# Four graph layers on one core: the first transposition of each group by VectorE 32x32 blocks and a DMA round trip

## The reference

```python
h = relu(layernorm(x))
# phase 0, two layers: u = (h @ (W_left h)^T above and on the diagonal, h @ (W_right h)^T below) / sqrt(384)
#   h = relu(LN(normalised(exp(u) * adj) @ (h W_lin^T + b)))
# phases 1 and 2, attention, 12 heads of 32:
#   out = softmax(q k^T / sqrt(384) + bias(adj)) v Wo^T + bo
# phase 3, two layers: a = softmax(h h^T / sqrt(384)) * adj, normalised
#   ctx = upper(a) (h Wl^T) + diag(a) (h Ws^T) + lower(a) (h Wr^T);  h = relu(LN(ctx))
x = x + result
```

## Time and profile before

| what | value |
|---|---|
| median of 3 runs | 2790.49 us (2787.36 to 2801.08) |
| span of the profiled execution | 2789.9 us; the page gives no time around it |
| VectorE, ScalarE, GpSimd busy | 2039.2, 1286.7, 1455.7 us (73%, 46%, 52%) |
| DMA queue q1 | 157.88 MB, 17.3% of 16 engines' span, mean 57 GB/s |
| ScalarE's copy of a transposed group (L684, L1558) | 813 and 810 ns |
| GpSimd L1084 (`out`) and L1067 (`xb`), four per group | 865 and 609 ns each |

### The profile page before, as it was taken

One profiled execution on the slowest core, in us unless ns is written; L12 is line 12 of the kernel. 1 busy time (PEld: TensorE's weight loads), 2 busy tenths in 40 slices (PEclk: granted clock), 3 DMA queues, 4 the chain that ended last, 5 costly groups with the idle time before them and its releaser, 6 DMA issues.

```text
span 2789.9 us, 85742 instructions
## 1 busy us (share of the span) xinstructions
PE 2736.0 (98%) x34344; PEld 2535.4 (91%) x34344; DVE 2039.2 (73%) x4000; ACT 1286.7 (46%) x2069; POOL 1455.7 (52%) x2499
## 2 busy tenths in 40 slices
PE   9999999999999999999989999998999999999998
PEld 8999999999988999999889999998888888888887
DVE  5666666666687777777777777778667777777776
ACT  4343343433444444445444444444545545445453
POOL 2212221122225555555554555555677877778777
PEclk9999999999999999999999999999999999999999
DMA  3221111212112111111131111111112112111121
GB/s 122 77 83 41 63 61 41 83 41 67 58 55 85 49 49 49 52 52 49 39 107 46 52 49 49 49 49 64 39 39 75 38 41 72 38 62 51 38 75 35
DMA packets 116556, 159.19 MB, mean 57 GB/s; under 512 B 8048, under 2 KB 112368, under 8 KB 116464
## 3 DMA queue, kind: packets, MB, share of 16 engines
q1 hardware_dynamic: 116464, 157.88, 17.3%
HBM read 107.52 MB, written 50.33 MB: 57 GB/s over the span
## 4 chain that ended last, share of the span: by engine, by line
PE 90%; DVE 4%; POOL 2%; issue 2%; ACT 1%; DMA 1%; SPq 0%; POOLq 0%; DVEq 0%; ACTq 0%
PE ps L337 68%; PE ps L1863 3%; PE ps L1337 3%; PE ps L1319 3%; PE ps L935 3%; PE ps L1352 3%; PE ps L958 2%; PE ps L1841 2%; PE ps L871 2%; PE ps L1247 1%; PE ps L1780 1%; POOL wide L1511 1%; PE ps L1849 0%; DVE w_lo L409 0%; DVE wide L1198 0%
## 5 line engine op out<-in xcount | busy, mean ns | idle before, releaser
L337 PE MATMUL ps<-w_hi,split 128*128 128x384 f32 x4608 | 1267.1, 344 | 9.8 <-ACT wide L1113 5.3
L337 PEld LDWEIGHTS ps<-w_hi,split 128*128 128x128 f32 x4608 | 841.0, 189 | 28.7 <-ACT wide L1113 5.7
L337 PE MATMUL ps<-split,w_hi 128*128 128x256 f32 x4608 | 858.6, 282 | 0.6 <-ACT wide L682 0.6
L337 PE MATMUL ps<-w_lo,split 128*128 128x384 f32 x2304 | 780.2, 339 | 0.0
L337 PEld LDWEIGHTS ps<-split,w_hi 128*128 128x128 f32 x4608 | 719.7, 188 | 20.4 <-issue 19.6
L337 PE MATMUL ps<-split,w_lo 128*128 128x256 f32 x2304 | 583.2, 282 | 0.0
L337 PEld LDWEIGHTS ps<-w_lo,split 128*128 128x128 f32 x2304 | 434.9, 189 | 2.5 <-issue 2.1
L337 PEld LDWEIGHTS ps<-split,w_lo 128*128 128x128 f32 x2304 | 433.6, 188 | 1.3 <-issue 1.2
L1084 POOL TENSOR_TENSOR wide<-wide 128x192 f32<-128x192 f32 x256 | 214.0, 865 | 372.1 <-ACT wide L1147 372.1
L1511 POOL TENSOR_TENSOR wide<-wide,row 128x192 f32<-128x192 f32 x512 | 328.9, 676 | 22.2 <-ACT wide L1594 21.6
L651 POOL TENSOR_TENSOR rstd<-mv,pos_half 128x2 f32<-128x2 f32 x64 | 45.9, 725 | 439.4 <-DVE mv L835 439.4
(11 more groups left out here) (141 smaller groups left out, 4534.8 us busy)
## 6 DMA issues: line engine op xcount, KB each, us to landing
x_after<-wide SPq DMA_DIRECT2D x96, 384.0 KB, 2.5
xin<-x_after SPq DMA_DIRECT2D x96, 384.0 KB, 3.4
xin<-in_x SPq DMA_DIRECT2D x32, 384.0 KB, 4.1
wide<-in_x SPq DMA_DIRECT2D x32, 384.0 KB, 3.6
wide<-x_after SPq DMA_DIRECT2D x32, 384.0 KB, 4.1
out<-wide SPq DMA_DIRECT2D x32, 384.0 KB, 2.8
adjin<-in_adj SPq DMA_DIRECT2D x32, 256.0 KB, 3.7
w_raw<-in_w SPq DMA_DIRECT2D x3, 2304.0 KB, 11.4
```

The lines of the kernel that those rows point to most:

```text
L337: mm = nc.tensor.matmul(out, t if tokens_stay else w, w if tokens_stay else t, start=(k == 0), stop=(k == len(pairs) - 1))
```

## The change

Only the very first group of all is still transposed by PE (stage `first`). For every other group:

1. x is loaded in two DMAs (one per tile) in another order of rows: partition = graph and token within 32, so that tile t holds tokens 32 t to 32 t + 31 of each half; the mean and variance do not care. For attention x is loaded a second time for `xb`, in the old order.
2. `norm` writes h in chunks of 32 features into the place `m.normal()`.
3. VectorE's new stage `turn` transposes all 32x32 blocks of the 128x768 tile in one instruction, back into `xin`.
4. SP stores that tile to HBM (`bounce`), waits for it, and loads it back in four DMAs of 96 KB, one per quarter of the partitions, with the quarters in swapped places (rows of 768 bytes). That gives features on partitions: `hT0`.
5. `split_0` (and `hT` in attention) wait for that DMA and read `hT0` from SBUF. The PE stages `hT_0` and `hT`, and the ScalarE copies behind `hT_0`, are gone. `u_0` reads `hT0`.

```diff
+        def turn(s, i):
+            b = bufs[s]
+            dve.wait_ge(act_done[s], AC[s]("h", i))
+            nc.vector.transpose(b.turned, b.h_all).then_inc(dve_done[s], 1)
...
+    def swap_quarters(s, i):
...
+        sp.wait_ge(now.dve_done[s], now.DV[s]("turned", i))
+        sp.dma_start(g.bounce[s], g.turned[s][:]).then_inc(now.sems.bounced[s], 16)
+        sp.wait_ge(now.sems.bounced[s], 16 * (i + 1))
+        for k in range(QUARTERS):
+            rows = slice(k * HD, (k + 1) * HD)
+            sp.dma_start(now.bufs[s].hT0_rows[rows], g.bounce_quarter[s][k]).then_inc(now.sems.hT_in[s], 16)
...
+    def turn(i):
+        for s in range(STREAMS):
+            store_and_reload(s, i - 2)
+            swap_quarters(s, i)
+            tokens(s, i + 1)
+            adjacency(s, i)
...
         def hT(s, i):
             b = bufs[s]
 
-            act.wait_ge(pe_done[s], PE[s].all(i, ("hT", 0), ("q", 1), ("k", 1), ("v", 1)))
...
-            nc.scalar.activation(b.t_hi[:], b.ps_row2, ACT.Copy).then_inc(act_done[s], 1)
+            act.wait_ge(sems.hT_in[s], QUARTERS * 16 * (i + 1))
...
+            nc.scalar.activation(by_graph(b.t_hi), b.hT0, ACT.Copy).then_inc(act_done[s], 1)
...
-            nc.vector.tensor_tensor(b.t_lo[:], b.ps_row2, b.t_hi[:].bitcast(F32), ALU.subtract)\
+            nc.vector.tensor_tensor(by_graph(b.t_lo), b.hT0, by_graph(b.t_hi).bitcast(F32), ALU.subtract)\
...
-        def hT(s, i):
...
-            for c in range(C):
-                for t in range(T):
-                    mm = nc.tensor.transpose(b.ps_row2[:, c, t * P:(t + 1) * P],
-                                             b.h[:, t, c * P:(c + 1) * P], g.ident[:])
```

The loops now mix three iterations (stages with no, one or two primes), run from iteration 4 to 15 (`MIXED` = 4), and load, normalise and turn a group one iteration before its products. `tokens` waits at a boundary for the store of its own group alone. The lists of all loops and boundaries are new. The attention loop on PE and VectorE:

```diff
-    "q0.1' q1.1' q2.1' k0.1' k1.1' v0.1' v1.1' pt0.0' hT.0 pt1.0' k2a.1' pt2.0' k2bc.1' pv.0' "
-    "scores.1' out0.0' out1.0' q0.0 q1.0 q2.0 k0.0 k1.0 v0.0 v1.0 pt0.1' hT.1 pt1.1' k2a.0 pt2.1' "
-    "k2bc.0 pv.1' scores.0 out0.1' out1.1'",
+    "q0.1'' q1.1'' q2.1'' k0.1'' k1.1'' v0.1'' v1a.1'' pt0.0'' v1bc.1'' pt1.0'' pt2.0'' k2.1'' pv.0'' "
+    "scores.1'' out0.0'' out1.0'' q0.0' q1.0' q2.0' k0.0' k1.0' v0.0' v1a.0' pt0.1'' v1bc.0' pt1.1'' pt2.1'' "
+    "k2.0' pv.1'' scores.0' out0.1'' out1.1''",
...
-    "stat.0 abs.0' fac.0' v.1' hT.0 pv.0' s.1' soft.1' stat.1 abs.1' fac.1' v.0 hT.1 pv.1' s.0 "
-    "soft.0",
-    "bias.1' stat.0 bias.0 p.0' xb.1' out.0' stat.1 p.1' xb.0 out.1'",
+    "abs.0'' fac.0'' v.1'' turn.1' stat.0 hT.0' pv.0'' s.1'' soft.1'' abs.1'' fac.1'' turn.0 stat.1 v.0' "
+    "hT.1' pv.1'' s.0' soft.0'",
+    "bias.1'' bias.0' p.0'' stat.0 out.0'' xb.1'' p.1'' stat.1 xb.0' out.1''",
```

The loop of phase 3 on PE and VectorE begins so, and the beginning on VectorE:

```diff
+    "aT_1.1'' agg_1.0'' u_0.0' w20_1.1'' w21ab_1.1'' w00_0.0' w21c_1.1'' w01_0.0' w10_0.0' w11_0.0' u_0.1' "
...
+    "split_1.1'' soft_1.1'' sum_1.0'' diag_1.0'' att_1.1'' w2_1.0'' aT_1.0'' split_0.0' sum_1.1'' turn.1' "
+    "diag_1.1'' soft_0.0' agg_1.0'' aT_1.1'' w2_1.1'' split_0.1' att_0.0' ln_1.0'' soft_0.1' sum_0.0' "
...
-    "stat.0 w0 split_0.0 w1 stat.1 w2 soft_0.0 att_0.0 split_0.1 lin_0.0 sum_0.0 agg_0.0 w3 ln_0.0 "
+    "stat.0 turn.0 stat.1 split_0.0 w0 w1 w2 turn.1 soft_0.0 att_0.0 w3 split_0.1 lin_0.0 sum_0.0 stat.0+ "
```

More of the change, by code:

```diff
@@ L237, in __call__ @@
         turn = i + self.late[name]
-        if isinstance(turn, int) and turn in (0, ITER):
-            here = sum(self.late[n] == (turn > 0) for n in self.place if self.place[n] <= self.place[name])
-            return here + (ITER * len(self.place) - self.missing if turn else 0)
+        if isinstance(turn, int):
+            whole = sum(min(max(turn - late, 0), ITER) for late in self.late.values())
+            return whole + sum(place <= self.place[name] and 0 <= turn - self.late[n] < ITER
+                               for n, place in self.place.items())
         return turn * len(self.place) + (self.place[name] - self.missing)
@@ L452, in load_x, with adjacency @@
-    def load_x(s, i, of=phase):
-        if of > phase:
-            ph.x_free(sp, s, ITER - 1)
-        elif not isinstance(i, int) or i > 0:
-            ph.x_free(sp, s, i - 1)
-        sp.dma_start(g.xin[s][:], g.sources[of][0][i * STREAMS + s]).then_inc(g.x_in[of][s], 16)
-    def load(s, i, of=phase):
-        load_adj(s, i, of)
-        load_x(s, i, of)
+    def adjacency(s, i):
+        now = ph
+        if isinstance(i, int) and i >= ITER:
+            if nxt == len(phases):
+                return
+            now, i = phases[nxt], i - ITER
+            if i == 0:
+                ph.adj_free(sp, s, ITER - 1)
+        if later(i):
+            now.adj_free(sp, s, i - 1)
+        _, adj, kinds, _ = g.sources[now.phase]
+        sp.dma_start(g.adjin[s][:, 0:len(kinds)], adj[i * STREAMS + s][:, kinds[0]:kinds[-1] + 1:kinds.step])\
+            .then_inc(now.sems.adj_in[s], 16)
@@ new lines, in tokens @@
+    def tokens(s, i):
+        now, made = ph, phases[phase - 1] if phase else None
+        if isinstance(i, int) and i >= ITER:
+            if nxt == len(phases):
+                return
+            now, made, i = phases[nxt], ph, i - ITER
+            if i == 0:
+                ph.x_free(sp, s, ITER - 1)
+                sp.wait_ge(sems.bounced[s], 16 * ITER)
+        if later(i):
+            now.x_free(sp, s, i - 1)
+            sp.wait_ge(now.sems.bounced[s], 16 * i)
+        if made is not None:
+            sp.wait_ge(made.sems.stored[s], 16 * (i + 1) + 1)
+        source = g.sources[now.phase][3] if phase or not very_first(s, i) else g.first_source
+        for t in range(T):
+            sp.dma_start(g.xin[s][:, t], source[i * STREAMS + s][t]).then_inc(now.sems.x_in[s], 16)
@@ L479, in move_program @@
         matrix(1)
[L480 removed]
+        tokens(1, 0)
         matrix(2)
[L482 removed]
+        adjacency(0, 0)
         for dst, src in g.const_loads:
@@ L852, in layer, with first @@
                     f"sum_{l}": total, f"agg_{l}": agg, f"ln_{l}": ln}
-        return {"stat": stat, "gain": gain, "beta": beta, "out": out, **layer(0), **layer(1)}
+        return {"stat": stat, "turn": turn, "gain": gain, "beta": beta, "out": out, **layer(0), **layer(1)}
     def tensor_stages(pe):
+        def first(s, i):
+            b = bufs[s]
+            pe.wait_ge(g.first_tile, 1)
+            for t in range(T):
+                if t > 0:
+                    pe.wait_ge(act_done[s], AC[s]("h", i))
+                for c in range(C):
+                    mm = nc.tensor.transpose(b.rows[0][:, c, t * P:(t + 1) * P], b.h_rows[:, t, c * P:(c + 1) * P], g.ident[:])
+            mm.then_inc(g.first_hT, 1)
+            warm_up(g, BRIDGING)
         def layer(l):
@@ L1271, in stage @@
                         o_taken(s, i, 0)
+                        if started(i, before) and before_att is None:
+                            pe.wait_ge(before.act_done[s], before.AC[s]("z_1", ITER - 1))
                         weights_made(pe, g, phase, WQ, i)
@@ L1761, in layer @@
                     f"aT_{l}": aT, f"agg_{l}": agg, f"ln_{l}": ln}
-        return {"stat": stat, "out": out, **layer(0), **layer(1)}
+        return {"stat": stat, "turn": turn, "out": out, **layer(0), **layer(1)}
     def tensor_stages(pe):
```

350 lines of the change are left out of this document (190 added, 160 removed), and 329 rows, old and new, of tables (BEGINNING, BETWEEN, ENDING, GCN0_ORDERS).

## The result

The changed kernel takes 2804.32 us (median of 5; 2801.59 to 2810.98) against 2790.8 for the kernel before on the same chip: ratio 1.0046, interval 1.0027 to 1.0064. It is 0.5% slower; 2716 was forecast. The profiled execution has a span of 2809.2 us against 2789.9, so the traces show +19.3, where the forecast had -75.

The account below looks back on a forecast made before the run. PE, busy for 98% of the 2789.9 us span, was taken as the bound. 2789.9 - 83.8 + 5 + 0 + 3.3 + 0 = 2714.4, or 2715.0 against the runs' median; 2716 was stated, range 2695 to 2765.

Parts of the forecast that it names:

- Part 1: PE, all phases: 127 blocks of six transpositions go, at 0.66 us each, -83.8 us (bounds -72 and -95).
- Part 2: VectorE gains 127 block transpositions at 0.96 us; its attention loop still fits; +5 us for GpSimd's lateness (bounds 0 and +20).
- the clause on the graph stages: Graph stages: a third to a quarter of VectorE's time is empty, so the block transposition costs nothing in a gap.
- Part 3: Store and four reloads on SP take 6.5 us (bounds 5 and 10), fitting by 0.7 in the last stage: 0.
- Part 4: ScalarE loses 63 copies of 0.81 us; VectorE's t_lo with two SBUF sources stays at 0.96: nothing.
- Part 5: Start: first product +3.0 us, as w0 follows the split; second group's trip +0.3; bounds 2 and 9.
- Part 6: Boundaries between phases: new orders for some 400 stages may shrink or grow 32 us of idle time; 0, bounds -15 and +15.
- It doesn't do what it says: Rival, whole kernel: the round trip's small waits cost what PE saved, time within 0.5%; chance 0.05.
- VectorE took next to nothing from attention: Rival judged here: VectorE becomes the bound in attention, 2758 us (range 2736 to 2775); chance 0.14.
- the trip was not late in the last stage: Rival judged here: at 10 us the trip is late in the last stage, +45 us, 2760; chance 0.08.
- the block transposition does not work block by block: Rival judged here: VectorE's transposition works block by block at 3.9 us, making the kernel slower, 2873 us; chance 0.09.
- the marks named ahead: Signs: 762 transpositions fewer, half-round 16.7, turn at most 0.96, trip 6.5, PE 100% in last stage, first product near 15 us.

Follow-up runs that it names:

- c3_turn_twice: c3_final with VectorE's block transposition issued twice for every group, in all four phases: 2791.29 us, ratio 0.9995.
- x3_order0: The changed kernel with two pairs exchanged in phase 0's lists: hT_1.1 ahead of norm.1, split_1.1 ahead of turn.1; 2802.93 us, ratio 1.0033.
- x4_trip_long: x1_adj_first with one more store to another place in DRAM, waited for, ahead of each trip's own store: 2813.92 us, ratio 1.0065.
- x1_adj_first: The changed kernel with the adjacency's load ahead of the store-and-reload trip and the tokens in each turn of the load program: 2774.44 us, ratio 0.9937.
- c4_cast_order: c3_final with both sides of the first cast in phases 0 and 3 walked in another order: 2746.52 us, ratio 0.9832.
- x2_start: The changed kernel with VectorE's list of the beginning altered, w0 ahead of split_0.0 and stat.1: 2806.3 us, ratio 1.0049.
- c3_final: x1_adj_first plus reordered lists, both first groups transposed on PE, trip before store out of phase 0, one token source corrected: 2743.41 us, ratio 0.9825.

## Why the prediction was wrong

**Part 1 (PE's blocks, -83.8): right in size.** PE's starts give 0.60 us for a group's six transpositions in phase 0 (2.52 to 1.32 for two), 0.655 in attention (1.31 to nothing) and 0.68 in phase 3, against 0.66 taken: 31 x 0.60 + 64 x 0.655 + 32 x 0.68 = 82. In attention the median round fell by 1.33 us, against 1.32 from the blocks alone. The counts fell as forecast: 192 transpositions are left in each graph phase where 384 were, and none of the first kind in attention.

**Part 2 (VectorE in attention, +5): right.** `turn` takes 0.97 us where 0.96 was taken, and the half-round is 16.6 (from 1607.54 to 1624.10 below) where 16.68 was forecast; c3_turn_twice shows the spare time: one half-round grew by the whole 1.00 that was added, so it had nothing to spare, where 0.11 was counted, and the other took 1.0 without growing, where 1.7 was counted.

```profile
1607.54 1.75 DVE L1299 TENSOR_TENSOR wide<-ps,bias 128x1536 f32<-128x1536 f32 x1
1624.10 1.75 DVE L1299 TENSOR_TENSOR wide<-ps,bias 128x1536 f32<-128x1536 f32 x1
```

The Trainium skill, Vector Engine (DVE) Microarchitecture Reference, section 3.8, gave one element per cycle per lane for the block transposition; the trace agrees, as it costs what the two-source operation of the same size does. What failed in this part is the clause on the graph stages, "costs nothing there if the order leaves it in a gap". In phase 0 the order did not: `norm.1` and `turn.1` ahead of the second layer's copy and split cost 0.6 us for a round (x3_order0).

**Part 3 (the trip, 0): the step that failed.** The trip itself was no longer than worked out where it was tightest: in the last stage 5.9 us (median) from the store's issue to the last landing, where 6.5 was taken; 6.4 in attention and 8.1 in phase 0, inside the bounds of 5 and 10. PE never waited for it in loop 3, and x4_trip_long, whose trip is 2.3 us longer there, shows at least that much to spare, where the prediction had 0.7. What failed is one sentence: "Behind the swap SP has `tokens` and `adjacency`, which GpSimd needs later than that." It compared the wrong two times. The adjacency was held above all by the trip's first wait, for VectorE's turn (SP stood 9.5 us at L521 in the rows above), and not by the trip alone, and GpSimd takes its stages in a written order, so that the sums which PE's aggregation needs stood behind an adjacency that nobody needed yet. x1_adj_first, which changes this alone, gives its price: 1.5 us for a round of phase 3 and more at the boundaries, 30 us in the medians.

**Part 4 (copies, nothing): wrong in a detail.** The first split's cast reads the transposed tile by graph and takes 943 ns, not the 560 of the earlier trace rows (559 there). It costs little: c4_cast_order took 1.2 us off loop 0 and left loop 3 as it was (665.1 against 665.0).

**Part 5 (start, +3.3): the term that was mis-sized.** `start` and `first8` grew by 8.8 us although the two rounds in them should have saved 2.6. Two steps failed. "stat.1 and split_0.0 ahead of w0" was priced as if stat.1 had its tokens; it waited 9.90 us for them, until 14.98. And the second group's trip was put at 7 us behind a turn that ends at 18.6; the turn ended at 25.0, since VectorE had the matrices before it, and the trip took 8.0 us, 4.4 of them for the store behind the start's loads. Of these the second decides: x2_start cured the first alone, and nothing was gained. Undone for that group, all of it came back.

**Part 6 (boundaries, 0, bounds -15 and +15): outside its bounds.** Outside the loops the forecast is -11.6 (12 rounds' blocks would be -15.8, + 3.3, + 0.9 of the 5) and the traces show +32.9, 44.5 over. The start is 8.1 of it, the rest 36.4. x1_adj_first took 14.6 of that back, the trip ahead of the store out of phase 0 another 5.4.

**The account.** Between the forecast (-75.5) and the traces (+19.3) lie 94.8 us: loop 3 (forecast -17.8, measured +11.8) 29.6; loop 0 (-15.8, -1.1) 14.7; the two attention stretches (-30.3, -24.4) 5.9; everything else 44.5. c3_final has 61.8 of it back. Still open are 33: the stretch from phase 0 into attention is 153.9 where 140 were forecast, loop 0 is 7 longer, and the rest is spread over the end and the other boundaries. In loop 0, where 0.6 us for a round is missing, 0.4 stand in the 256-column products. From one of them to the next, or to a 384-column product, PE's starts are 0.117 us apart; from one to an aggregation (L1059) 0.21, and from the first of them behind an aggregation or a small transposition to the second 0.20 to 0.23. The new order goes from these products to an aggregation three times for a round instead of twice; no run has tested whether that is the cause. The orders of c3_final were not given to the kernel before, so its gain is not parted from theirs; in the graph loops, where PE was busy for 100.00 of 100 before, they had little to win.

**The rivals.** "It doesn't do what it says: the round trip costs what PE saved, in many small waits" (chance 0.05) is what happened, and its time was right, though not for the reason that it gives: the waits were not the trip's but those of other stages behind it in two queues. VectorE took next to nothing from attention, whose round fell by the 1.33 forecast, though one half-round has no room left; the trip was not late in the last stage; the block transposition does not work block by block (0.97 us, where that rival had 3.9). Of the marks named ahead, three came out (762 blocks fewer, half-rounds of 16.71 and 16.55, turn 0.97), the trip was shorter (5.9), and three gave the alarm: PE at 95.8% in the last stage, the first product at 20.70, the boundaries by more than 15 us.

**The rule on transpositions of 128x128.** The Trainium skill, VectorE: DVE Perf Modes, section Rules for kernel authors, sends a 128x128 transposition to TensorE where a PSUM destination will do. With the lists as they came the rule held by 0.5%. With them mended, and with both streams' first groups back on TensorE, the measurement is against it by 1.75% for this kernel, whose TensorE is busy for 98%.

## What to carry to other kernels

A step that waits must be priced for every instruction that stands behind it in its queue, from the moment at which the queue reaches it and not from the moment at which its own work starts; loads that wait for nothing belong ahead of it. Where engines run written orders, taking work off the busiest one also takes away cover: look for each short stage of another engine that waits for a third and stands ahead of something that the busy engine needs. Price the loop and the ends apart: a round trip through HBM was free in both graph loops and left most of the gain standing in attention, and a trip 2 to 5 us longer cost 28 us in the start and the boundaries, so leave it out for the first groups, where the queue is full (9.8 us here).

## What the runs showed of the hardware

**Cast and access pattern.** In phase 0, 128 x 768 elements of float32 are cast within SBUF in 560 ns from one row to one row, in 943 with the source walked as 3 x 4 x 64 and the destination one row, and in 551 with the source one row and the destination walked as 4 x 3 x 64. The Trainium skill, VectorE: DVE Perf Modes, section What auto-detection actually checks, asks for outermost counts that are both even, or equal, for the two-elements-per-cycle mode; the three durations agree. In phase 3 the counts alone don't settle it, since the third form took about 960 ns there in about half of the cases.

**The clock after a pause.** In the changed kernel PE starts its first products at 20.70 after 11.1 us of idle; up to 24.25 they start 0.21 us apart and the granted clock of 20 to 24 is 0.50, the 1.2 GHz level, and from 24.4 on they start 0.12 apart. On the boundary the granted clock of 810 to 820 is 0.69, a mix of the 1.2 and 2.4 GHz levels (starts 0.21 apart up to 816, 0.12 from 817.2), behind ten us in which PE was busy for 5.88. So part of what a stretch with waits costs is slower products behind it, some 1.5 us at the start (16 steps, each 0.09 longer).

```profile
800.00:810.00 10.00, 5.88 (x80) 4.58 (x84) 6.51 (x21) 3.01 (x7) 2.38 (x6) 0.97 0.07 24
810.00:820.00 10.00, 8.79 (x57) 7.57 (x58) 7.68 (x16) 4.31 (x8) 1.31 (x1) 0.69 0.18 47
820.00:830.00 10.00, 10.00 (x118) 9.60 (x117) 4.94 (x12) 3.38 (x4) 1.71 (x1) 1.00 0.44 139
```

**One store, four prices.** The same 384 KB store lands after 2.3 us in phase 3, 3.1 in attention and 4.5 in phase 0, where reloads of 384 KB and adjacencies of 256 KB stand with it in the queue; at the start, with 8.2 MB in 40 us, it took 6.3 (x2_start). In x4_trip_long, where SP issues it only when another store has landed, it takes 2.3 in every phase (median), so the difference lies in what stands ahead of it.
